# Weight block sums made once in DRAM, and three pairs of CMS chunks by seven products

## What is computed

```
q, k, v = x @ Wq, x @ Wk, x @ Wv
attn_out = softmax(q k^T / sqrt(512)) v @ Wp + bp
cms_out  = gelu(attn_out @ cW1 + cb1) @ cW2 + cb2 + one_hot(target_codes)   # cW1 512x2048, cW2 2048x512
modifier = gelu(concat(attn_out, cms_out) @ mW1 + mb1) @ mW2 + mb2         # mW1 1024x2048
x = clip(x + cms_out + modifier, 0, 1)
# adapter, weights chosen by a role per sequence
h = gelu(x @ W_down[role] + b_down) @ W_up[role] + b_up                     # 512 -> 256 -> 512
x = layernorm(x + h) * gamma + beta
```

## Time and profile before

| | |
|---|---|
| median of 3 runs | 2160.12 us |
| profiled execution | 2156.44 us, its span 2154.8 us, mean granted clock 0.998 |
| TensorE busy | 2105.6 us, 9256 matmuls |
| VectorE, ScalarE, GpSimd busy | 1537.7, 1042.1, 598.7 us |
| DMA | 146.41 MB, 68 GB/s over the span |

### The profile page before, as it was taken

How to read it: one execution, slowest core, us unless ns; L and a number is a source line. 1 busy time by engine, 2 the same in 40 slices (tenths; PEclk the granted TensorE clock), 3 DMA queues, 4 the chain that set the end, 5 groups by cost and what they waited for, 6 DMA issues and landing times.

```text
span 2154.8 us, 24846 instructions
## 1 busy us (share of the span) xinstructions
PE 2105.6 (98%) x9256; PEld 1724.7 (80%) x9256; DVE 1537.7 (71%) x1923; ACT 1042.1 (48%) x1527; POOL 598.7 (28%) x620
## 2 busy tenths in 40 slices
PE   8999999999999999999999999999999999999997
PEld 6888887888788887888877888788887888878884
DVE  4366678776867668876776766977686866787676
ACT  5264445454446444544554544444454644454444
POOL 1001136452001113655000111655400011355420
PEclk9999999999999999999999999999999999999999
DMA  8101131212202112221312111321130211311211
GB/s 304 40 10 59 59 88 49 59 48 78 100 20 88 59 59 69 59 59 59 116 41 88 40 59 42 96 59 59 40 127 20 102 46 59 88 50 59 59 59 39
DMA packets 125767, 146.41 MB, mean 68 GB/s; under 512 B 5952, under 2 KB 100160, under 8 KB 123728
## 3 DMA queue, kind: packets, MB, share of 16 engines
q1 hardware_dynamic: 122912, 130.05, 18.9%
q0 software_dynamic: 1504, 8.49, 1.9%
q10 hardware_dynamic: 1232, 6.29, 0.7%
HBM read 123.84 MB, written 12.58 MB: 63 GB/s over the span
## 4 chain that ended last, share of the span: by engine, by line
PE 85%; DVE 10%; ACT 2%; issue 2%; DMA 0%; SPq 0%; ACTq 0%; DVEq 0%
PE bank L615 28%; PE bank L617 28%; PE bank L616 28%; DVE ring L1321 2%; DVE vc L1363 2%; DVE pc L1493 1%; DVE xa L1358 1%; DVE lsum L1695 1%; ACT ring L955 1%; ACT raw L1098 0%; PE bank L923 0%; DVE xs L1700 0%; DVE xs L1653 0%; DVE xs L1685 0%; DVE raw L1439 0%
## 5 line engine op out<-in xcount | busy, mean ns | idle before, releaser
L1321 DVE TENSOR_TENSOR ring<-stage,ring 128x1024 fp32r<-128x1024 f32 (+1 forms) x312 | 363.4, 1176 | 103.8 <-ACT ring L955 103.6
L551 POOL TENSOR_TENSOR stage<-stage 128x256 f32<-128x256 f32 x120 | 106.3, 886 | 1122.1 <-DMA stage<-cms_w 904.5
L615 PE MATMUL bank<-ph_hi,ring 128*128 128x512 f32 x1048 | 410.6, 392 | 5.4 <-issue 2.4
L617 PE MATMUL bank<-ph_hi,ring 128*128 128x512 f32 x1048 | 407.9, 389 | 0.0
L616 PE MATMUL bank<-ph_lo,ring 128*128 128x512 f32 x1048 | 407.9, 389 | 0.0
L615 PE MATMUL bank<-xa,ring 128*128 128x512 f32 x1016 | 396.0, 390 | 2.9 <-DVE xs L1653 2.1
L617 PE MATMUL bank<-xa,ring 128*128 128x512 f32 x1016 | 395.3, 389 | 0.0
L616 PE MATMUL bank<-xa,ring 128*128 128x512 f32 x1016 | 395.3, 389 | 0.0
L955 ACT ACTIVATE ring<-stage 128x1024 fp32r<-128x1024 f32 (+1 forms) x312 | 296.3, 970 | 111.7 <-PE bank L617 78.3
L615 PEld LDWEIGHTS bank<-ph_hi,ring 128*128 128x128 f32 x1048 | 196.7, 188 | 53.7 <-issue 7.2
L617 PEld LDWEIGHTS bank<-ph_hi,ring 128*128 128x128 f32 x1048 | 196.7, 188 | 41.0
(11 more groups left out here) (159 smaller groups left out, 3139.6 us busy)
## 6 DMA issues: line engine op xcount, KB each, us to landing
stage<-mod_w SPq DMA_DIRECT2D x128, 256.0 KB, 3.4
stage<-cms_w SPq DMA_DIRECT2D x36, 512.0 KB, 3.6
stage<-mod_w SPq DMA_DIRECT2D x32, 512.0 KB, 4.9
stage<-cms_w SPq DMA_DIRECT2D x56, 256.0 KB, 4.3
fold_staging<-fold_w SPq DMA_DIRECT2D x16, 512.0 KB, 5.2
stage<-folded SPq DMA_DIRECT2D x16, 512.0 KB, 4.3
xs<-pc POOLq DMA_DIRECT2D x8, 1024.0 KB, 8.3
stage<-ada_w SPq DMA_DIRECT2D x16, 512.0 KB, 3.6
```

Source lines behind the costliest of these rows:

```text
L551: pool.tensor_tensor(part(S1), part(S2), part(A22), ALU.add).then_inc(sums_ready, 1)
L615: pe.matmul(dst, lh, rh, start=start and n == 0, stop=False, skip_group_check=not start)
L617: done = pe.matmul(dst, ll, rh, start=False, stop=n == last, skip_group_check=not start)
L1321: dve.tensor_tensor(ring_part(key, 1), staged(key), f32(ring_part(key, 0)), ALU.subtract).then_inc(w_lo, 1)
```

## The change

The kernel gets two more DRAM tensors: `ready_w`, which holds for each layer 30 weight pieces with all seven blocks (A, C, D), and `ready_pair`, with three double pieces E for each layer (seven blocks of 128x512). They are filled during rounds 0 and 1:

- SP copies blocks from the weight tensors to the places of the seven blocks (`prepare`: seven DMAs for a piece, four for a D piece), DRAM to DRAM.
- GpSimd adds in DRAM with accumulating DMAs: three in a first step (`sum_once`), two in a second (`sum_twice`), each step after a wait for the step before. GpSimd's `sums` on the staging buffers are gone.
- The pieces are portioned out: five portions of three pieces ahead of round 0 (four of them, 12 pieces, are in SP's queue before the first load of an A piece, one after the first two loads), then one to three pieces per slot over rounds 0 and 1 (`PER_SLOT`). A slot's copies are in up to three parts, put between the loads. The first step of a portion stands two slots after its number in GpSimd's queue, the second three slots.

The loads of A, C, D (slots 8 to 14) and E pieces bring all seven blocks in one DMA. All A pieces are in buffer 0 now; E takes buffers 1 and 2 together.

The down products of CMS chunks 0 and 1, 2 and 3, 4 and 5 are made by seven products for each pair (`pair_product`: 7 x 2 tiles x 2 halves x 3 passes), spread over an odd slot (Q1 and Q5 of its own pair, Q7, Q4, Q2 of the pair before) and an even one (Q3 and Q6). Chunks 6 and 7 stay plain. GpSimd makes the T sums of raw tiles in these slots too (`pair_sum`), the odd chunk's raw tiles are in `raw_odd` (in free tiles of `vc`), and VectorE adds the products 128x1024 at a time (`pair_add`). The slots have new orders on all engines; slot 7 has its own (`cms_last`), in which the splits of the last D piece and of slot 8's C piece stand earlier.

```diff
+EARLY = (3, 3, 3, 3, 3)
+PER_SLOT = CH // 2 * (1, 2) + (3, 3, 3, 2, 2, 0, 0, 0) + CH // 2 * (1, 2) + (3, 3, 3, 3, 2, 0, 0, 0)
...
+            def load_ready(key):
+                layer, at = key[0] // 2, STAGE_OF[key]
+                to = stage_pair if key[1] == "E" else stage[at]
+                s = READY_IN[(layer, *key[1:])]
+                sp.wait_ge(w_lo, STAGE_FREE[key])
+                sp.wait_ge(prepared[batch_sem(s)], 16 * batch_count(s, lambda kind: 2))
+                sp.dma_start(to[:, :, :], ready_piece(layer, *key[1:]).rearrange("b p n -> p b n")).then_inc(stage_in[at], 16)
+
+            def prepare(s, part=0, parts=1):
+                under = ((A11, 0, 0), (A12, 0, 1), (S4, 0, 1), (S1, 1, 0), (S3, 1, 0), (S2, 1, 1), (A22, 1, 1))
...
+                    else:
+                        halves = piece.rearrange("p (k m n) -> p k m n", k=4, m=2)
+                        for block, m, k in under:
+                            sp.dma_start(to[UP_AT[block], :, :].rearrange("p (k n) -> p k n", k=2),
+                                         halves[:, 2 * k:2 * k + 2, m, :]).then_inc(copied[slot], 16)
...
             for r in range(ROUNDS):
                 load((r, "P"), cms_w[2 * (r // 2) * CH, :, :])
+                if r == 0:
+                    sp.wait_ge(fold_out[1], 16 * LAYERS)
+                    for early in range(-len(EARLY), -1):
+                        prepare(early)
                 load_up(r, 1)
-                load_down(r, 0)
+                load_pair(r, 1)
+                if r == 0:
+                    prepare(-1)
...
                 for n in range(1, SLOTS):
+                    prepare_next(r, n - 1, 0)
                     if n + 1 < SLOTS:
                         load_up(r, n + 1)
...
+                    prepare_next(r, n - 1, 1)
                     if n >= CH:
                         load_down(r, n)
+                    prepare_next(r, n - 1, 2)
                     if CH <= n + 1 < SLOTS:
                         load_up(r, n + 1, "C")
...
+            def sum_once(s):
+                slot = batch_sem(s)
+                pool.wait_ge(copied[slot], 16 * batch_count(s, COPIES.get))
+                for layer, kind, n in BATCHES_READY[s]:
+                    w, at = ready_piece(layer, kind, n), UP_AT if kind in ("A", "C") else DOWN_AT
+                    for block, more in ((S1, A22), (S3, A11), (S4, A22)):
+                        pool.dma_start(rows(w, at[block]), rows(w, at[more]), accum_op=ALU.add, max_dma_last_dim=8192).then_inc(summed_once[slot], 16)
...
+            def pair_even(r, n):          # TensorE
+                i = n // 2 - 1
+                up(r, n, Q5)
+                up(r, n, Q1)
+                pair_product(r, i, Q3)
+                up(r, n, Q6)
+                up(r, n, Q2)
+                up(r, n, Q3)
+                up(r, n, Q7)
+                pair_product(r, i, Q6)
+                up(r, n, Q4)
...
+            def pair_even(r, n):          # VectorE
+                i = n // 2 - 1
+                pair_add(r, i, Q5)
+                split_lo((r, "E", n - 1, 3))
+                split_lo((r, "A", n, 1))
+                pair_split_lo(r, i, T3, 0)
+                pair_split_lo(r, i, B21, 1)
+                pair_split_lo(r, i, T2, 0)
+                pair_split_lo(r, i, T3, 1)
+                pair_add(r, i, Q3)
+                pair_split_lo(r, i, T2, 1)
+                combine(r, n, C12)
+                pair_split_lo(r, i, T4, 0)
+                combine(r, n, C22)
+                split_lo((r, "A", n + 1, 0))
+                pair_add(r, i, Q6)
+                pair_split_lo(r, i, T4, 1)
+                if paired(n):
+                    pair_split_lo(r, i + 1, B11, 0)
...
```

More of the change, by code:

```diff
@@ L156, in staged_up @@
     def staged_up(r, n):
[L157 removed]
+        pieces.append(((r, "A", n), 0))
         if n >= CH:
@@ L184, in weight_stream @@
         plain(r, "P", 0)
-        for n in range(CH):
-            if n and n - 1 not in LASTS:
-                down(r, n - 1)
-            up(r, n + 1, 0)
-            if n in LASTS:
-                down(r, n)
-            up(r, n + 1, 1)
+        up(r, 1, 0)
+        ops.append((r, "A", 1, 1))
+        for n in range(1, CH - 1):
+            if n % 2 == 0:
+                ops.append((r, "E", n - 1, 3))
+            if n > 1:
+                ops.append((r, "A", n, 1))
+            if n % 2:
+                pair_first(r, n)
+                ops.append((r, "E", n, 1))
+            up(r, n + 1, 0)
+            if n % 2:
+                ops.append((r, "E", n, 2))
+        ops.append((r, "A", CH - 1, 1))
+        down(r, CH - 2)
+        staged_up(r, CH)
+        ops.append((r, "A", CH, 0))
+        down(r, CH - 1)
+        ops += [(r, "C", CH, 0), (r, "A", CH, 1), (r, "C", CH, 1)]
         up(r, CH + 1, 0)
@@ L1579, in slot @@
                     down_add(r, n - 1, 0, m)
                 hidden_lo(r, n, 0)
-                if last:
-                    for m in range(KT):
-                        down_add(r, n - 1, 1, m)
-                    hidden_lo(r, n, 3)
-                    split_lo((r, "D", n))
-                    hidden_lo(r, n, 1)
-                    combine(r, n, C12)
-                    hidden_lo(r, n, 2)
-                else:
-                    combine(r, n, C12)
-                    hidden_lo(r, n, 1)
-                    down_add(r, n - 1, 1, 0)
@@ L1593, in slot @@
-                up_lo(r, n + 1, 1)
-                if not last:
-                    for m in range(1, KT):
-                        down_add(r, n - 1, 1, m)
+                for m in range(KT):
+                    down_add(r, n - 1, 1, m)
+                hidden_lo(r, n, 3)
+                split_lo((r, "C", n + 1, 0))
+                hidden_lo(r, n, 1)
+                combine(r, n, C12)
+                hidden_lo(r, n, 2)
+                split_lo((r, "A", n + 1, 1))
+                split_lo((r, "C", n + 1, 1))
```

583 lines of the change are left out of this document (444 added, 139 removed).

## The result

The changed kernel takes 2236.9 us (median of 4 runs, 2229.9 to 2240.4) where the kernel before, run beside it, takes 2159.7: +77.2 us, ratio 1.036 with the interval 1.0345 to 1.0381. The forecast was 2137, range 2114 to 2172; the result is outside it, on the slow side.

A forecast was written before the change was run, and what follows sets the result against it. It took the number of matmuls on TensorE, busy 98%, as the bound. -32.6 + 6 - 8 + 5 + 0 + 9 = -20.6 us against 2156.4 gave 2135.8, stated as 2137 us for the median, range 2114 to 2172.

The forecast's parts named there:

- Part 1: CMS chunk pairs: 144 fewer matmuls at 0.2267 us each, -32.6 us, with nothing hiding it.
- Part 2: VectorE and ScalarE in the pair slots: even slot nearly VectorE bound, 0.5 us in each of 12, +6 us (0 to +18).
- Part 3: CMS end: without GpSimd's sums on the shared SBUF port, VectorE runs faster and TensorE idles less, -8 us (0 to -11.9).
- Part 4: DMAs of larger loads and preparation, in three places: start +5 us, CMS slots 0, modifier slots of rounds 0 and 1 +9.
- the start: Before round 0: copies and accumulations ahead of A1's load, landing at 142 to 155 us, +5 us (0 to +68).
- the CMS slots: A loads into one buffer land in about 5.5 us and fit with under 1 us to spare: 0 (to +1 in each of 28).
- nine such slots at 1 us: Modifier slots 9 to 13 of rounds 0 and 1: 25 to 33 us of DMA for 28.6, +9 us (0 to +40).
- the second: Rival: middle slots of rounds 0 and 1 bound by DMA and GpSimd's queue, 27 + 14 in place of 9, 2168 us; chance 0.15.
- The third: Rival: at the start, half-rate copies delay A1 to 207 us, ScalarE stands 68 us, about 2199 us in all; chance 0.18.
- The sign I asked for: Rounds 2 and 3, without preparation, each 8 to 10 us shorter than now, or the forecast is wrong.
- The sign for Part 4: Slots 9 to 13 of rounds 0 and 1: DMA share above 0.9 and TensorE idle about 1 us a slot.

The follow-up runs named there:

- copies_only: Changed kernel without the 330 accumulating DMAs, loads waiting for the copies only; 2123.5 us, ratio 0.985 to the kernel before.
- pairs_only: Changed kernel with four-block loads and GpSimd's weight sums in SBUF, nothing prepared in DRAM; 2168.2 us, ratio 1.006 to the kernel before.
- noprep: Changed kernel without all preparation copies and accumulations, same-size loads read from the weight tensors; 2119.0 us, ratio 0.983 to the kernel before.
- pool_order: Changed kernel with GpSimd's last early accumulation steps behind the raw-tile sums of slots 1, 2 and 4; 2236.5 us, ratio 1.037 to the kernel before.
- accum_tiny: Changed kernel with all 330 accumulating DMAs kept in order but cut to 8 or 16 KB each; 2123.0 us, ratio 0.984 to the kernel before.
- early_load: Changed kernel with pool_order's order, copies behind each slot's last load, only two early portions ahead of A1's load; 2190.2 us, ratio 1.015 to the kernel before.
- cms_ready: Changed kernel with modifier and round 0 CMS pieces summed in SBUF, CMS pieces for rounds 1 to 3 prepared in DRAM behind modifier-slot loads; 2129.4 us, ratio 0.986.

## Why the prediction was wrong

- **Part 1, -32.6: right.** 9112 matmuls, and 2074.5 us busy in `copies_only`, 31.1 below.
- **Part 2, +6: too high.** The pair slots of round 2 (1311 to 1426 us) of the changed kernel have 0.26 us of idle time in 115: the walk through the even slot was sound and its half microsecond not needed.
- **Part 3, -8: some -5.** The same 48 us of the CMS end in rounds 2 and 3:

```profile
1426.00:1474.00 48.00, 46.60 (x202) 37.32 (x201) 38.05 (x45) 23.02 (x31) 4.90 (x4) 1.00 0.39 101
...
1934.00:1982.00 48.00, 46.24 (x201) 36.99 (x199) 37.20 (x46) 21.47 (x28) 3.85 (x4) 1.00 0.39 102
```

  1.4 and 1.8 us idle, against 2.5 and 3.1 in rounds 2 and 3 before, and the 128x1024 operations in them take 1.22 us, where the earlier trace rows had 1.6 to 2.7. That is what the rule I cited from the Trainium skill (GPSIMD Engine Reference, section 1, Specifications) says of the shared SBUF interfaces, and in `pairs_only`, with the sums back, VectorE's same instructions are busy 91 us longer. The gain there is some 1.2 us a round, not 2, about 5 in all. Parts 1 to 3 together were forecast at -34.6 and measured at -37.5: 32.6 and 5, with nothing lost in the pairs.
- **Part 4 failed: +14 forecast, 115 measured** (changed kernel less `noprep`). Its three places: the start, 11.5 us over `noprep` (I had +5, to +68; A1 was there at 153.4, within "142 to 155"); the CMS slots, which I had at nothing ("fits with under 1 us to spare: 0"), and which cost 34.6 + 20.9 = 55.5 us (in round 0 first as the wait of 24.8 us behind GpSimd's accumulations, which `pool_order` turned into waits for loads; between 170 and 297 us TensorE works 94.75 us, where the kernel before had 127.00); and "nine such slots at 1 us" of the modifier stage, which took 33 to 37 us in round 0 and 30 to 33 in round 1, from one C split to the next, instead of 28.6, some 45 us in ten slots. Rounds 0 and 1 together are 108 us longer than `noprep`'s (577.9 + 549.0 less 509.6 + 509.3).

The step that failed is the pricing of the waits for loads in Part 4, in two terms: the CMS slots at 0 because a landing of "about 5.5 us" fits, and slots 9 to 13 at 1 us each by a sum, "the engines get 7 to 14 us of copies, 10 of loads and 5 to 12 of accumulations: 25 to 33 us for 28.6". The rates were not at fault: the copies ran at 287 GB/s (66 MB in the 230 us by which SP's queue of `copies_only` holds the engines longer than `noprep`'s; I had 265) and cost 4.5 us, and the accumulations ran at 197 GB/s (47.2 MB in 240 us). That I had 201 is partly luck, since my row was an addition from SBUF to SBUF. Wrong was that a load is issued on time and keeps its own 5.5 us until the sum reaches the slot. At a share of 0.72 ScalarE stood 7 to 11 us at C loads of round 0, because such a load has only some 6 us between its buffer coming free and its split; in these it came late in both ways, issued behind copies that held SP for up to 17.8 us (the text's 9 us for 21 issues should have been 12.6 by its own 0.6) or split some 13 us after the issue, beside what stood in both queues. The text had even cited the rule for it (the Trainium skill, DMA: Bandwidth & Descriptors, "Issuing engines are not separate DMA queues": all transfers run on the same 16 engines and interleave), and used it for the sum of a slot, not for the delay of one load in it. Its evidence was thin too: in the row with the share of 0.99 the loads had landed and only GpSimd's addition ran, so it could not show what two queues do to each other. The runs agree with the rule: `accum_tiny` against the changed kernel differs in nothing but the bytes on the other queue, and by 111 us.

A second omission is the clock. After stalls TensorE's granted clock was 0.50 in one window and 0.95 over round 0; I had no term for it. It is an estimated 30 us of the 115 at most (2104.1 less 2074.5 us of busy time for the same matmuls, in which the ends of matmuls before stalls are counted too).

Of the rivals, the second (middle slots bound by DMA) was the right mechanism, too small in both stages: 3 us in each modifier slot where it was 4 to 8 in round 0 and 1.5 to 5 in round 1, and 14 us in the CMS slots where it was 55. It named GpSimd's issues as a part, which `accum_tiny` shows to be free. The third named the copies before A1; copies cost 4.5 us in all, and `early_load` shows that a late start is not even added to the rest. The sign I asked for, rounds 2 and 3 shorter by 8 to 10 us each, came as said (9.4, 8.2), so it confirmed Parts 1 to 3 and said nothing on the part that decided. The sign for Part 4, a share above 0.9 in slots 9 to 13, did not come: it was 0.72, with far more idle time than 1 us a slot, so the slots were not short of engine time but of loads on time.

Open: whether the accumulations would cost as much without the copies; how a load's delay arises inside the engines (whether by turns between queues or by reads and writes of DRAM), and why the ten pieces per round of `cms_ready` cost nothing at a share of 0.58 in 380 to 590 us. Its loads in these slots are 512 KB, not 896, and fewer bytes are accumulated; no run changes one without the other.

## What to carry to other kernels

Price a background transfer by what it does to the foreground load with the least slack, not by whether the sum of all fits the slot: a share below 1 says nothing when a load has 6 us from free buffer to use (0.72 here with 21 us of TensorE's time lost in 210, and 0.82 with 5 lost once the loads went first). Put foreground loads ahead of background copies in the same queue (43 us here), and give background work the stages whose loads are small. And an accumulating DMA from DRAM to DRAM holds the engines nearly twice as long as a plain copy of the same rows, so move sums there only for data that is used again and where no load is waiting.

## What the runs showed of the hardware

- DRAM to DRAM on GpSimd's queue: 47.2 MB in 240 us of all 16 engines when accumulating (197 GB/s), in 129 us as plain copies (366 GB/s). Cutting the descriptors to a quarter raised the packets from 12,544 to 29,824 and the share from 12.6% to 14.3%, and GpSimd then stood 115.5 us before accumulating DMAs, which it had not with the longer descriptors.
- The rows that these DMAs are written in did not set their packets: rows of 2 KB and of 8 KB of the same contiguous block gave the same 12,544.
- A load of 896 KB landed in a median of 5.4 us with copies alone in the stretch, and of 7.3 to 11.4 us with copies and accumulations (`copies_only` in 340 to 600 us; the changed kernel in 920 to 1180 and 340 to 600), and seven copies of 128 KB took SP 4.5 us to issue at best and 17.8 us at worst.
- 66 MB of copies (336 of 128 KB, 84 of 256 KB) on SP's queue cost 4.5 us when nothing accumulated beside them, though they stood in front of loads; with the accumulations beside them the same order cost 43 us more than loads first.
